# Pairs of heads in the last attention: scores on two row halves of TensorE, without zero padding

## What is computed

```python
q = jnp.einsum('btc,hdc->bhtd', x, Wq)
k = jnp.einsum('btc,hdc->bhtd', x, Wk)
...
v = jnp.einsum('bthe,bted->bhtd', mix_v, proj_v)      # the 2 chosen of 8 experts, by sigmoid gates
scores = jnp.einsum('bhid,bhjd->bhij', q * DH ** -0.5, k)
probs = jax.nn.softmax(scores, axis=-1)
attn = jnp.einsum('bhij,bhjd->bihd', probs, v)
...
res = jnp.einsum('bthe,bthd,efd->bthf', mask_o, attn, Wo)
return res.sum(axis=2)
```

## Time and profile before

| | |
|---|---|
| median of 3 runs | 3291.48 us |
| the profiled execution's own time | 3297.39 us |
| its span | 3295.5 us |
| PE (TensorE) busy | 2666.0 us, 81% |
| DVE (VectorE) busy | 1837.7 us, 56% |
| ACT (ScalarE) busy | 1446.3 us, 44% |
| POOL (GpSimd) busy | 1020.1 us, 31% |
| mean granted TensorE clock | 0.897 of full speed |

### The profile page before, as it was taken

One profiled execution on the slowest core, in us unless ns is written; L12 is line 12 of the kernel. 1 busy time (PEld: TensorE's weight loads), 2 busy tenths in 40 slices (PEclk: granted clock), 3 DMA queues, 4 the chain that ended last, 5 costly groups with the idle time before them and its releaser, 6 DMA issues.

```text
span 3295.5 us, 36665 instructions
## 1 busy us (share of the span) xinstructions
PE 2666.0 (81%) x12668; PEld 1520.5 (46%) x12668; DVE 1837.7 (56%) x4565; ACT 1446.3 (44%) x2310; POOL 1020.1 (31%) x423
## 2 busy tenths in 40 slices
PE   0565889899948996888898878898879798888899
PEld 0522222232225653465574356475356476346467
DVE  8455012121131114865894875795775796685777
ACT  3033567677811222632453541453551354451354
POOL 1023000000011113630751640571460590260292
PEclk9987898999969996889998889998889898789999
DMA  1054842533141111020001011000002000002000
GB/s 55 0 186 156 119 58 53 82 48 44 63 167 41 45 41 39 1 76 25 20 1 39 1 57 43 21 1 14 26 7 93 20 1 7 26 1 93 0 1 7
DMA packets 88476, 146.54 MB, mean 44 GB/s; under 512 B 16724, under 2 KB 58840, under 8 KB 88248
## 3 DMA queue, kind: packets, MB, share of 16 engines
q1 hardware_dynamic: 80760, 134.57, 15.7%
q0 software_dynamic: 7504, 9.35, 1.5%
HBM read 121.17 MB, written 22.88 MB: 44 GB/s over the span
## 4 chain that ended last, share of the span: by engine, by line
PE 61%; DVE 20%; ACT 7%; issue 7%; DMA 3%; SPq 1%; POOL 1%; DVEq 0%; ACTq 0%; POOLq 0%
PE ps L1489 7%; PE ps L1649 6%; PE ps L1640 6%; PE ps L1256 4%; PE ps L1267 4%; PE ps L1519 3%; PE ps L1627 3%; ACT sb_arena L918 3%; PE ps L1424 2%; PE ps L1589 2%; PE ps L1490 2%; DVE sb_arena L2239 2%; PE ps L1443 2%; PE ps L1437 2%; PE ps L1569 2%
## 5 line engine op out<-in xcount | busy, mean ns | idle before, releaser
L918 ACT ACTIVATE sb_arena<-ps 128x1024 f32<-128x1024 f32 x416 | 402.8, 1021 | 177.8 <-PE ps L1256 170.9
L2239 DVE MAX8 sb_arena<-sb_arena 128x8 f32<-128x60 f32 (+1 forms) x1728 | 247.6, 206 | 175.3 <-ACT sb_arena L1013 175.1
L1489 PE MATMUL ps<-sb_arena 128*128 128x512 f32 (+1 forms) x512 | 296.4, 666 | 25.3 <-ACT sb_arena L1013 13.3
L1256 PE MATMUL ps<-sb_arena 96*128 96x512 bf16 x832 | 241.6, 398 | 56.2 <-issue 37.7
L1649 PE MATMUL ps<-sb_arena 128*128 128x512 f32 x512 | 279.4, 630 | 2.7 <-ACT sb_arena L1087 2.7
L688 POOL TENSOR_TENSOR sb_arena<-sb_arena 128x1024 f32<-128x1024 f32 x96 | 223.7, 2330 | 164.8 <-DVEq L2347 153.9
L802 POOL TENSOR_TENSOR sb_arena<-sb_arena 128x1601 f32<-128x1601 f32 x56 | 173.9, 3105 | 314.8 <-DVE sb_arena L2227 314.8
L1640 PE MATMUL ps<-sb_arena 128*128 128x64 f32 x2048 | 260.9, 271 | 0.0
L1640 PEld LDWEIGHTS ps<-sb_arena 128*128 128x128 f32 x2048 | 252.9, 194 | 0.3
L1100 ACT ACTIVATE sb_arena<-ps,sb_arena 128x512 f32<-128x512 f32 x256 | 175.6, 686 | 170.8 <-DVE sb_arena L2388 167.6
L690 POOL TENSOR_TENSOR sb_arena<-sb_arena 128x1024 f32<-128x1024 f32 x84 | 229.9, 2737 | 6.6
(11 more groups left out here) (343 smaller groups left out, 4798.8 us busy)
## 6 DMA issues: line engine op xcount, KB each, us to landing
sb_arena<-in_ctxT SPq DMA_DIRECT2D x13, 1601.0 KB, 7.4
sb_arena<-k_spill SPq DMA_DIRECT2D x96, 208.0 KB, 8.1
sb_arena<-in_dft SPq DMA_DIRECT2D x5, 2048.0 KB, 7.9
k_spill<-sb_arena SPq DMA_DIRECT2D x12, 832.0 KB, 5.2
sb_arena<-in_w SPq DMA_DIRECT2D x16, 512.0 KB, 6.5
sb_arena<-in_idft SPq DMA_DIRECT2D x4, 2048.0 KB, 9.6
sb_arena<-in_wf SPq DMA_DIRECT2D x8, 1024.0 KB, 13.0
sb_arena<-q_spill SPq DMA_DIRECT2D x96, 64.0 KB, 9.2
```

The lines of the kernel that those rows point to most:

```text
L918: A(probs0[:, 2 * (m % 4):2 * (m % 4) + 2, :], ps[:, 2 * (m % 2):2 * (m % 2) + 2, :], ACT.Exp).then_inc(pair_probs, 1)
L1256: ins = mm(ps[:, 2 * (m % 2) + i, :], k_stack[0:NSPLIT, h, k * P:(k + 1) * P], q_stack[0:NSPLIT, h, :], start=True, stop=True)
L1489: mm(ps[:, j, 0:w], q1z[:, h, t * P:(t + 1) * P], kT1[:, c0:c0 + w], start=True, stop=False)
L2239: ins = V.max(cand[:, n % 2, 8 * j:8 * j + 8], s_sb[n % 4][:, c0:c0 + w])
```

## The change

Queries are kept as `q2`, two heads in the two halves of the rows like the keys. The zero halves, the two memsets of GpSimd and the semaphore `q2_clear` go. ScalarE copies a pair of heads out in one operation instead of two. The loop goes in steps s of two heads j = 0, 1 at one query tile t: 32 steps per batch, four to a pair of heads. The two scores of a step are products over 64 rows, one on each half of TensorE's rows, into two neighbouring banks. VectorE takes one maximum over both banks (128 x 2 from 128 x 2 x 512). In TensorE's queue step s has the two scores, then the eight transposes of step s-1, then the two values of step s-2. `pT2` has four buffers instead of two. The head outputs of a pair lie in one bank. VectorE's head_sum and head_add move: the order is in the last part of the diff.

```diff
-        q2z = at(o, [H2, SEQ]); o += H2 * SEQ
+        q2 = at(o, [H2 // 2, SEQ]); o += H2 // 2 * SEQ
-        pT2 = at(o, [2, SEQ]); o += 2 * SEQ
+        pT2 = at(o, [4, SEQ]); o += 4 * SEQ
...
-                pool.wait_ge(f_done, nth(b, f_done, TILES))
-                nc.gpsimd.memset(q2z[0:D2, 1:H2:2, :], 0.0).then_inc(q2_clear, 1)
-                nc.gpsimd.memset(q2z[D2:P, 0:H2:2, :], 0.0).then_inc(q2_clear, 1)
-
-                pool.wait_ge(q2_clear, nth(b, q2_clear, 2))
...
-                    for j in range(2):
-                        r = slice(j * D2, (j + 1) * D2)
-                        ins = A(q2z[r, 2 * i + j, :], ps[r, (2 * i) % 4, :], ACT.Copy, scale=D2 ** -0.5)
-                    ins.then_inc(qk2_ready, 1)
+                    A(q2[:, i, :], ps[:, (2 * i) % 4, :], ACT.Copy, scale=D2 ** -0.5).then_inc(qk2_ready, 1)
...
+                for s in range(NG // 2 + 1):
+                    for j in range(2):
+                        if s >= 1:
+                            m = 2 * s - 2 + j
+                            act.wait_ge(p2T_done, nth(b, p2T_done, m + 1))
+                            if m >= 4:
+                                act.wait_ge(o2_done, nth(b, o2_done, m - 3))
+                            A(pT2[:, m % 4, :], ps[:, 2 + m % 2, :], ACT.Copy).then_inc(p2T_ready, 1)
+                        if s < NG // 2:
+                            n, t, h = 2 * s + j, s % TILES, s // TILES * 2 + j
+                            act.wait_ge(s2_max, nth(b, s2_max, s + 1))
+                            if n >= 4:
+                                act.wait_ge(p2T_done, nth(b, p2T_done, n - 3))
+                            A(p2[:, n % 4, :], ps[:, S2_BANKS[n % 4], :], ACT.Exp, bias=nmax2[:, t, h:h + 1],
+                              accum_out=sums2[:, t, h:h + 1]).then_inc(p2_ready, 1)
...
-                    if t == 0 and h >= 2:
-                        pe.wait_ge(gated, nth(b, gated, h - 1))
+                    if t == 0 and j == 0 and pair >= 2:
+                        pe.wait_ge(gated, nth(b, gated, 2 * pair - 2))
...
+                for s in range(NG // 2 + 2):
+                    if s < NG // 2:
+                        pair, t = s // TILES, s % TILES
+                        for j in range(2):
+                            n, half = 2 * s + j, slice(j * D2, (j + 1) * D2)
+                            if n >= 4:
+                                pe.wait_ge(p2_ready, nth(b, p2_ready, n - 3))
+                            mm(ps[:, S2_BANKS[n % 4], :], q2[half, pair, t * P:(t + 1) * P], kT2[half, pair, :],
+                               start=True, stop=True).then_inc(s2_done, 1)
+                    for j in range(2):
+                        if 1 <= s < NG // 2 + 1:
+                            turn_p2(2 * s - 2 + j)
+                    for j in range(2):
+                        if s >= 2:
+                            value2(2 * s - 4 + j)
...
-                    dve.wait_ge(p2_ready, nth(b, p2_ready, TILES * (h + 1)))
+                    dve.wait_ge(p2_ready, nth(b, p2_ready, 2 * TILES * (pair + 1)))
...
-                    dve.wait_ge(o2_done, nth(b, o2_done, TILES * (h + 1)))
+                    dve.wait_ge(o2_done, nth(b, o2_done, 2 * TILES * (pair + 1)))
...
-                for n in range(NG):
-                    h, t = n // TILES, n % TILES
-                    dve.wait_ge(s2_done, nth(b, s2_done, n + 1))
-                    V.tensor_reduce(nmax2[:, t, h:h + 1], ps[:, S2_BANKS[n % 4], :], AX.X, ALU.max, negate=True).then_inc(s2_max, 1)
-                    if h >= 2 and t == 0:
-                        head_sum(h - 2)
-                    if h >= 2 and t == 2:
-                        head_add(h - 2)
-                for h in range(H2 - 2, H2):
-                    head_sum(h)
-                    head_add(h)
+                for s in range(NG // 2):
+                    pair, t, bank = s // TILES, s % TILES, S2_BANKS[2 * s % 4]
+                    dve.wait_ge(s2_done, nth(b, s2_done, 2 * s + 2))
+                    V.tensor_reduce(nmax2[:, t, 2 * pair:2 * pair + 2], ps[:, bank:bank + 2, :], AX.X, ALU.max, negate=True).then_inc(s2_max, 1)
+                    if pair >= 2 and t == 0:
+                        head_add(2 * pair - 3)
+                    if pair >= 1 and t == 2:
+                        head_sum(2 * pair - 2)
+                    if pair >= 1 and t == 3:
+                        head_add(2 * pair - 2)
+                        head_sum(2 * pair - 1)
+                head_add(H2 - 3)
+                head_sum(H2 - 2)
+                head_add(H2 - 2)
+                head_sum(H2 - 1)
```

More of the change, by code:

```diff
@@ L472, in program @@
         f_done = sem("f_done", 4)
-        q2_clear = sem("q2_clear", 2)
         qk2_done = sem("qk2_done", 16)
@@ L485, in program @@
         s2_done = sem("s2_done", 64)
-        s2_max = sem("s2_max", 64)
+        s2_max = sem("s2_max", 32)
         p2_ready = sem("p2_ready", 64)
@@ L1078, in _ @@
                 A(sig_v, gate_v, ACT.Sigmoid).then_inc(sig_ready, 1)
-                act.wait_ge(q2_clear, nth(b, q2_clear, 2))
                 for i in range(H2 // 2):
                     act.wait_ge(qk2_done, nth(b, qk2_done, 2 * i + 1))
-                    for j in range(2):
-                        r = slice(j * D2, (j + 1) * D2)
-                        ins = A(q2z[r, 2 * i + j, :], ps[r, (2 * i) % 4, :], ACT.Copy, scale=D2 ** -0.5)
-                    ins.then_inc(qk2_ready, 1)
+                    A(q2[:, i, :], ps[:, (2 * i) % 4, :], ACT.Copy, scale=D2 ** -0.5).then_inc(qk2_ready, 1)
@@ L1630, in value2 @@
                 def value2(n):
-                    h, t = n // TILES, n % TILES
+                    s, j = n // 2, n % 2
+                    pair, t = s // TILES, s % TILES
+                    h = 2 * pair + j
                     if n == 0:
@@ L1636, in value2 @@
                     pe.wait_ge(p2T_ready, nth(b, p2T_ready, n + 1))
-                    if t == 0 and h >= 2:
-                        pe.wait_ge(gated, nth(b, gated, h - 1))
-                    for j in range(TILES):
-                        ins = mm(ps[:, 4 + h % 2, t * D2:(t + 1) * D2], pT2[:, n % 2, j * P:(j + 1) * P],
-                                 v2[:, j, h * D2:(h + 1) * D2], start=(j == 0), stop=(j == TILES - 1))
-                    ins.then_inc(o2_done, 1)
[L1644 to L1653, removed]
+                    if t == 0 and j == 0 and pair >= 2:
+                        pe.wait_ge(gated, nth(b, gated, 2 * pair - 2))
+                    for k in range(TILES):
+                        ins = mm(ps[:, 4 + pair % 2, (j * TILES + t) * D2:(j * TILES + t + 1) * D2], pT2[:, n % 4, k * P:(k + 1) * P],
+                                 v2[:, k, h * D2:(h + 1) * D2], start=(k == 0), stop=(k == TILES - 1))
+                    ins.then_inc(o2_done, 1)
+                for s in range(NG // 2 + 2):
+                    if s < NG // 2:
+                        pair, t = s // TILES, s % TILES
+                        for j in range(2):
[10 more added lines that the diff above has]
+                            value2(2 * s - 4 + j)
                 for t in range(TILES + 1):
@@ L2353, in head_sum @@
                 def head_sum(h):
-                    dve.wait_ge(p2_ready, nth(b, p2_ready, TILES * (h + 1)))
+                    pair, j = h // 2, h % 2
+                    o_at = j * TILES * D2
+                    dve.wait_ge(p2_ready, nth(b, p2_ready, 2 * TILES * (pair + 1)))
                     link(V.reciprocal(rs2[:, :, h], sums2[:, :, h]))
                     link(V.tensor_tensor(gates_o[:, :, h, :], gates_o[:, :, h, :], per(rs2[:, :, h], E2), ALU.mult))
-                    dve.wait_ge(o2_done, nth(b, o2_done, TILES * (h + 1)))
+                    dve.wait_ge(o2_done, nth(b, o2_done, 2 * TILES * (pair + 1)))
                     if h == H2 - 1:
@@ L2365, in head_sum @@
                                 V.tensor_tensor(z_tmp[:, t, :].rearrange("p (e d) -> p e d", d=D2),
-                                                ps[:, 4 + h % 2, t * D2:(t + 1) * D2].unsqueeze(1).to_broadcast(by_expert),
+                                                ps[:, 4 + pair % 2, o_at + t * D2:o_at + (t + 1) * D2].unsqueeze(1).to_broadcast(by_expert),
                                                 gates_o[:, t, h, :].unsqueeze(2).to_broadcast(by_expert), ALU.mult).then_inc(gated, 1)
@@ L2371, in head_sum @@
                         return
-                    src = ps[:, 4 + h % 2, 0:TILES * D2].rearrange("p (t d) -> p t d", d=D2).unsqueeze(2).to_broadcast(shape)
+                    src = ps[:, 4 + pair % 2, o_at:o_at + TILES * D2].rearrange("p (t d) -> p t d", d=D2).unsqueeze(2).to_broadcast(shape)
                     gate = gates_o[:, :, h, :].unsqueeze(3).to_broadcast(shape)
```

## The result

The changed kernel takes 3336.22 us (median of 4 runs, 3331.84 to 3343.15), against 3290.65 us before (4 runs, 3287.58 to 3298.54): 1.0137 times as long, 95% interval [1.0112, 1.0162]. That is 45.6 us slower, and 16 us beyond the range's upper end. The profiled execution has a span of 3341.4 us, against 3295.5 before.

What follows compares the result with a forecast made beforehand. TensorE was taken to bound the loop, with VectorE close behind. Profiled 3297.4 + 8.8 (longer loops) - 10.1 (memsets gone) = 3296.1 us, or 3290.2 for the median; range 3268 to 3320.

Steps and rivals of the forecast that it cites:

- Rival (c): Attention loop: TensorE's gaps lower its granted clock, at 0.9 costing 12 us in all, 3302 us; chance 0.10.
- the 0.95: Attention loop: a granted clock under this value was named as a sign that the prediction is wrong.
- The row halves: TensorE's scores: two heads' products on two row halves overlap, 1.2 us per pair instead of 1.82.
- Rival (b): TensorE's scores: the halves don't overlap, 2.0 us instead of 1.2 per step, 50 us in all, 3340 us; chance 0.12.
- The maximum over 1024: VectorE: one maximum for two heads lasts 1.22 us, giving VectorE almost nothing, 0.06 us a step.
- The circle without GpSimd: TensorE and VectorE waiting on each other in the loop: 16.6 us per pair of heads, against 17.5 before.
- The VectorE work behind the last maximum: End of the loop: three head_adds and two head_sums take 12.1 us, against 4.9 before.
- The circle beside GpSimd: Head pairs 3 to 5, while GpSimd mixes values: its holds add 2.7 us, making 19.3 us per pair.
- rival (d): Beside GpSimd: head_adds and gate products wait a whole GpSimd operation each, 14 us in all, 3304 us; chance 0.10.
- rival (a): Faster: the gate product doesn't meet GpSimd, 22 us, 3269, or row-half switching is free, 16 us, 3275; chance 0.28.
- The last interval of the circle: VectorE, t = 3 to next t = 0: head_add, head_sum and maximum take 5.97 us without GpSimd.
- The zero padding: Ahead of the loop: without GpSimd's memsets the third normalisation falls from 2.94 to 0.41 us, 10.1 us won in all.

Runs made afterwards that it cites:

- fill: Changed kernel plus three idle float32 products ahead of the transposes at the three places of TensorE's long wait; 3287.56 us, 1.0041 of the kernel before.
- memset: Changed kernel with GpSimd's two memsets and ScalarE's wait for them put back; 3354.15 us, 1.0222 of the kernel before.
- spread: Changed kernel with VectorE's four long operations one per step instead of two at t = 3; 3244.72 us, 0.9902 of the kernel before.
- full: Changed kernel with scores over all 128 rows, zero padding, memsets and the two query copies put back; 3367.86 us, 1.0256 of the kernel before.

## Why the prediction was wrong

The step that failed is the clock. The sum gave it no term behind the first pair of heads: the pairs beside GpSimd stood in it at 19.3 us, at full clock. Rival (c) said that "TensorE would have gaps of 1.5 to 2.5 us in each pair", priced them at "3 per batch or more, 12 in all", and had a chance of 0.10. In the runs the gaps beside GpSimd were 2.25 to 4.21 us (one of twelve was 1.52), the clock of the loop was 0.87, under the 0.95 that the prediction named as a sign of being wrong, and this cost 11.9 us per loop, 48 in all: four times the rival's price. Point by point:

- The row halves: 1.2 us for a pair of scores; 1.06 measured (1664.24 to 1665.30). That is 0.15 more than one product over 128 rows (0.91), overlap and switching together, where two of those take 1.82. Rival (b) is out.
- The maximum over 1024: 1.22, as forecast.
- The circle without GpSimd: 16.6 forecast and measured. The VectorE work behind the last maximum: 12.1, against 12.15 measured.
- The circle beside GpSimd: 19.3. With the clock kept up (fill) it is 19.2 to 19.6 in all three pairs, counted as the forecast counts, from the last maximum of one pair to that of the next; the whole loop is 145.9 against the 146.4 summed. The gate product waits for the whole resumed operation (1.71 in the row above, 2.14 at most), as described, so rival (d) is out, and rival (a) as far as it rests on the gate product. This sum was right for full clock. As it ran, the three pairs of the first loop took 23.6 us each, counted so (by their first maxima 23.7, 24.0 and 20.7).
- The clock: the sum held what refuted its own assumption. The last interval of the circle, from the maximum at t = 3 to the one at t = 0, was 5.97 us without GpSimd. With the 1.75 of the gate product and the 0.55 of the head_add it is 8.3 (measured 1662.23 to 1670.60: 8.4). TensorE has 3.76 us of work in it, so the circle's own terms leave a gap of 4.5 us, most of it in one piece (3.50 in the row of 1672.68). The rival's 1.5 to 2.5 us are what the circle leaves without GpSimd (5.97 - 3.76 = 2.2). It also took the clock from the search stage, by mean busy shares, as a tenth over a few us. In the runs it is a halving for 7 to 17 us behind each long wait.
- The zero padding: 4 x 2.53 = 10.1 forecast. The normalisation's 2.94 is gone, and memset brings it back at the same place; with what follows up to the first maximum it is 13.2. The span outside the loops fell by only 7 us in the profiled executions; two executions of the changed kernel differ by 6 there.

With the clock's 48 us added, the forecast of 3290 becomes 3338, against 3336.22 measured. Part of that closeness is luck: the four loops at full clock were forecast 2 us too long and the rest of the span 3 us too short. In spread order both gains come through, and the kernel is about 1% faster than before.

## What to carry to other kernels

Where a change takes work off TensorE and another engine becomes the bound, write down TensorE's longest single wait, all locks and holds included, and not only its mean busy share: here each wait of 2.25 to 4.21 us cost some 4 us more behind it (11.9 / 3), while behind the shorter ones, of 1.52 us at most, the clock stayed up. On the engine that is late, put its long operations one per step; that change of order alone turned a kernel 1.4 to 1.7% slower than before into one 1% faster. Filler products in the wait are a good test of whether the clock is the cause, and a worse cure than taking the wait away.

## What the hardware showed that was not expected

- Two products of 64 x 512 float32 on the two row halves share 1.06 us from the first's start to the next work, where one over 128 rows takes 0.91.
- In the changed loop (TensorE busy 138.08 of 158.30 us) one wait of 2.25 to 4.21 us was followed by 7 to 17 us at 1.2 GHz, in eleven of twelve places; in full 2.04 us was enough. Behind waits of 1.52 and 1.01 us the clock stayed at 2.4 GHz.
- A VectorE head_add that GpSimd has held holds GpSimd's next operation for 1.9 us in turn (1.93 to 3.86, 2.36 to 4.28), and the next small VectorE product of two SBUF operands pays for it: 0.19 becomes 1.71, or 1.00 with a maximum between them.
